# Mamba's state loop in a four-image network: the input of both halves in one VectorE instruction, two sets of tiles, new turn tables

## Chip, cores, metric

The kernel runs on one core of one Trainium2 chip. The metric is the time of one execution on the device, in microseconds. The time before is 1499.15 us, the median of 3 runs (1498.88 to 1500.82).

## What is computed

The input is a batch of 4 images of 512 tokens with 128 features, in float32. Eight residual layers follow each other: a state-space mixer (L0), a feed-forward layer, a Mamba block, a mixture of 8 experts with GELU, a linear attention, a ternary feed-forward layer, a second state-space scan, and a gated mixture of 8 experts. Each is applied as x = x + layer(layernorm(x)). What the change touches is the Mamba block, cut here to its state loop:

```python
D_STATE = 16; D_INNER = 256
u, z = split(layernorm(x) @ W_in); u = silu(conv1d(u) + conv_b)
dt, Bm, Cm = split(u @ W_xproj)            # widths 8, 16, 16
dt = softplus(dt @ W_dt + b_dt)
A = -exp(A_log)                            # (256, 16)
dA = exp(dt[..., None] * A)                # decay, for each token, channel, state
dBu = (dt * u)[..., None] * Bm[:, :, None, :]   # input of the state
h = dA_t * h + dBu_t                       # over the tokens
y_t = sum over n of h[:, n] * C_t[n]
out = x + ((y + u * D) * silu(z)) @ W_out
```

## The kernel before

**Streams.** Four images are worked off in two streams: images 0 and 2 are stream 0, images 1 and 3 are stream 1. Each stream has its own tiles (suffix `s`) and four of the eight PSUM banks (`bank(s, k)`, L465). Each engine's program is written as Python generators, one per layer and image, which yield between pieces of work. `walk` (L483) asks the two streams' generators for their next piece in the order of a fixed table: `RUNS[engine]` (L100 to L142) holds run lengths, alternately for stream 0 and stream 1. So the order of all instructions on an engine's queue is written out ahead, the two streams are interleaved by the table, and a piece that has to wait holds up everything behind it on that engine. The table `"sp"` does the same for the expert loads, stores and gathers of the SyncE queue, and `expert_loads` (L164) reads from it in which order the ring of four expert buffers is filled.

**Mamba, by engine.** The channels lie on the partitions in two halves j = 0, 1 of 128, the 512 tokens on the free axis. Per image, 16 iterations n (one for each state) follow the preparation:

- TensorE (`mamba`, from L1620): broadcasts row n of Bm to bank 2 and row n of Cm to bank 3 (L1659, a 96-row selection matmul in bf16). `sum_states` (L1638) adds the weighted states of both halves onto banks 0 and 1 with the identity as weights (L1642), over all n.
- ScalarE (`mamba`, from L782): copies bank 2 to the tile MT in SBUF (L814), and computes the decays of the two halves into CV (L821, Exp with the scale A).
- GpSimd (`mamba`, L614): multiplies MT with dt*u of half 1 into BIG2[1] (L624).
- VectorE (`mamba`, from L1192): multiplies bank 2 with dt*u of half 0 into BIG2[0] (L1222), then runs the scans of both halves into UP (L1230), then multiplies both with bank 3 into BIG2[2:4] (L1237, 128x1024 in one instruction, the PSUM row broadcast over the halves).

There is one set of decay tiles (CV) and one of input tiles (BIG2[0:2]). So the exponential of state n + 1 waits for the scan of state n of the same half, and the input of state n + 1 for that scan too. The semaphores: `m_bc` counts TensorE's rows, `m_bs` the copies, `m_da` the decays, `m_d1` GpSimd's products, `m_scan` VectorE's four instructions of an iteration, `m_ya` the sums.

**Around it.** The layers that can run beside Mamba are the L0 mixer of the other stream (VectorE convolutions L1050 to L1053, gates L1084; TensorE L1529) and the experts (TensorE L1739 up and L1712 down, ScalarE's GELU L862, VectorE's results L1314, GpSimd's indirect DMAs L639 for the scatter and L646 for the gather). GpSimd also computes the norms' power (L587). ScalarE loads a function table whenever the function set changes (Exp, Ln, Silu, Gelu, Sigmoid).

## Time and profile before

| what | value |
|---|---|
| runs | 1499.15 us median, 1498.88 to 1500.82 |
| profiled execution, its own time | 1508.51 us |
| its span, first to last instruction | 1506.4 us |
| mean granted TensorE clock | 0.886 |
| instructions | 16451 |
| HBM traffic | 109.31 MB read, 15.07 MB written |

The profile is of one execution. A busy time is the time in which an engine has an instruction under way; times of instructions are starts and durations by the hardware profiler, and durations of neighbours on VectorE overlap by some tens of ns. "Idle before" is the time in which the engine stood still ahead of such an instruction, put down to what released it last. L numbers are lines of the kernel before. The tile names leave buffer numbers out: `big` is BIG1 or BIG2, `ps` is PSUM, `mt`, `cv`, `up`, `q` are MT, CV, UP and the split rows. The stretches of the Mamba loops below run from the first to the last scan: image 0's from 216.3 to 316.8 us, image 1's from 259.7 to 389.2, image 2's from 879.6 to 990.4, image 3's from 1033.3 to 1116.6.

### The profile page before, as it was taken

What the parts mean: (1) busy time and instruction counts of PE and PEld (TensorE: products, weight loads), DVE (VectorE), ACT (ScalarE), POOL (GpSimd) and SP (SyncE); (2) the same over time, 40 slices, a digit from 0 to 9 for tenths busy, and PEclk for the clock granted to TensorE, in tenths of its full rate; (3) what the DMA queues carried; (4) which work ended last, traced back from release to release, by engine and by line L of the source; (5) the groups of instructions that cost most, each with busy time, mean ns of one, the idle gap of its engine ahead of it and who ended that gap; (6) DMA issues with size and microseconds to landing.
All of it is one profiled execution on the core that took longest, in us unless ns stands there. A gap on an engine that the chain in (4) does not pass through costs nothing.

```text
span 1506.4 us, 16451 instructions
## 1 busy us (share of the span) xinstructions
PE 1151.1 (76%) x5428; PEld 761.0 (51%) x5428; DVE 920.1 (61%) x2079; ACT 662.9 (44%) x1289; POOL 280.6 (19%) x261
## 2 busy tenths in 40 slices
PE   0988656667869989976897767755867999978774
PEld 0534522233757446666775423433635745547674
DVE  4575679998627384234484778987786355334432
ACT  1532267524634343452452476436943434443321
POOL 1200112425140201203202211213242020020222
PEclk9998767877989998989999868986988999988987
DMA  8000000003564000536540000003513600033763
GB/s 330 0 1 0 1 0 0 0 1 103 188 200 125 20 1 4 172 101 212 172 166 28 7 0 0 0 1 104 172 43 104 200 15 1 0 131 121 271 205 131
DMA packets 57641, 125.50 MB, mean 83 GB/s; under 512 B 5320, under 2 KB 38224, under 8 KB 57168
## 3 DMA queue, kind: packets, MB, share of 16 engines
q1 hardware_dynamic: 52880, 111.14, 22.5%
q0 software_dynamic: 4096, 8.40, 1.7%
q10 hardware_dynamic: 576, 4.87, 0.8%
q8 instruction: 45, 0.74, 0.2%
q14 instruction: 44, 0.36, 0.1%
HBM read 109.31 MB, written 15.07 MB: 83 GB/s over the span
## 4 chain that ended last, share of the span: by engine, by line
PE 46%; DVE 18%; ACT 13%; issue 9%; DMA 8%; POOL 5%; SPq 1%; DVEq 0%; another core or an unknown queue 0%; POOLq 0%; ACTq 0%
PE ps L1739 6%; PE ps L1801 5%; PE ps L1529 5%; DMA expert_ring<-in_e_dram 4%; PE ps L1477 4%; PE ps L1642 3%; PE ps L1712 3%; DVE up L1230 3%; PE ps L1771 2%; POOL slots_dram L639 2%; POOL up L646 2%; PE ps L1582 2%; PE ps L1839 1%; ACT big L862 1%; PE ps L1790 1%
## 5 line engine op out<-in xcount | busy, mean ns | idle before, releaser
L1739 PE MATMUL ps<-big,expert_ring 128*128 128x128 f32 x1440 | 200.1, 289 | 45.6 <-DMA expert_ring<-in_e_dram 18.1
L1739 PEld LDWEIGHTS ps<-big,expert_ring 128*128 128x128 f32 x1440 | 184.6, 201 | 66.7 <-issue 34.5
L587 POOL TENSOR_TENSOR rstd<-ve,nhalf 128x4 f32<-128x4 f32 x44 | 48.2, 1096 | 692.3 <-DVE ve L1024 548.0
L1230 DVE TENSOR_TENSOR_SCAN up<-cv,big 128x512 f32<-128x512 f32 x128 | 151.5, 1223 | 24.7 <-ACT cv L821 18.1
L1642 PE MATMUL ps<-big,consts 128*128 128x512 f32 x256 | 149.1, 713 | 2.2 <-DVE big L1237 2.2
L1712 PE MATMUL ps<-expert_ring,big 128*128 128x128 f32 x960 | 130.0, 279 | 11.5 <-DVE big L1350 6.4
L624 POOL TENSOR_TENSOR big<-big,mt 128x512 f32<-128x512 f32 x64 | 85.1, 1333 | 263.2 <-ACT mt L814 133.6
L1712 PEld LDWEIGHTS ps<-expert_ring,big 128*128 128x128 f32 x960 | 119.3, 194 | 18.4 <-DVE big L1350 7.1
L1659 PE MATMUL ps<-q,row_pick 96*128 96x512 bf16 x128 | 54.5, 441 | 89.3 <-DVE big L1237 57.4
L1801 PE MATMUL ps<-big,weights 128*128 128x512 f32 x256 | 116.1, 598 | 0.8 <-DVE big L1402 0.8
L859 ACT ACTIVATE key<-ps,expert_ring 128x128 f32<-128x128 f32 x240 | 68.6, 369 | 106.2 <-PE ps L1739 94.6
L1350 DVE SCALAR_TENSOR_TENSOR big<-ps,expert_ring,key 128x128 f32<-128x128 f32 x240 | 67.5, 344 | 67.2 <-PE ps L1739 48.8
L1477 PE MATMUL ps<-weights,big 128*128 128x128 f32 x608 | 83.6, 298 | 16.3 <-DVE big L1244 10.5
L821 ACT ACTIVATE cv<-big,nega 128x512 f32<-128x512 f32 x128 | 88.1, 716 | 16.6 <-DVE up L1230 16.0
L1477 PEld LDWEIGHTS ps<-weights,big 128*128 128x128 f32 x608 | 79.5, 210 | 29.1 <-DVE big L1244 13.7
L639 POOL DMA_INDIRECT slots_dram<-cv,key x64 | 66.8, 1044 | 122.2 <-DVE key L1301 105.5
L814 ACT ACTIVATE mt<-ps 128x512 f32<-128x512 f32 x64 | 38.2, 599 | 114.6 <-PE ps L1659 104.8
L862 ACT ACTIVATE big<-ps,expert_ring 128x128 f32<-128x128 f32 x240 | 68.3, 376 | 44.6 <-PE ps L1739 44.4
L646 POOL DMA_INDIRECT up<-results_dram,key x64 | 62.1, 970 | 126.2 <-DMA results_dram<-mt 101.4
L1642 PEld LDWEIGHTS ps<-big,consts 128*128 128x128 f32 x256 | 58.5, 230 | 50.0 <-issue 42.6
L1659 PEld LDWEIGHTS ps<-q,row_pick 96*128 96x128 bf16 x128 | 13.4, 106 | 135.9 <-DVE big L1237 74.0
L1237 DVE TENSOR_TENSOR big<-up,ps 128x1024 f32<-128x1024 f32 x64 | 77.6, 1213 | 7.0 <-PE ps L1642 6.1
(249 smaller groups left out, 1990.7 us busy)
## 6 DMA issues: line engine op xcount, KB each, us to landing
expert_ring<-in_e_dram SPq DMA_DIRECT2D x60, 836.0 KB
expert_ring<-in_e_dram SPq DMA_DIRECT2D x60, 578.0 KB
big<-slots_dram SPq DMA_DIRECT2D x24, 256.0 KB, 3.2
results_dram<-mt SPq DMA_DIRECT2D x24, 256.0 KB, 4.5
weights<-in_w_dram ACTq DMA_DIRECT2D x1, 3072.0 KB, 14.8
slots_dram<-big SPq DMA_DIRECT2D x2, 960.0 KB, 16.0
weights<-in_w_dram SPq DMA_DIRECT2D x1, 1600.0 KB, 13.4
big<-slots_dram SPq DMA_DIRECT2D x8, 192.0 KB, 3.8
```

The source lines that it names most:

```text
L624: pool.tensor_tensor(BIG2[s][:, 1, :], BIG1[s][:, 3, :], MT[s][:, 0:T], ALU.mult).then_inc(m_d1[s], 1)
L639: pool.indirect_dma_start(xs_d[k], bass.IndirectOffsetOnAxis(ap=posu[s][:, j:j + 1], axis=0), XH[s][:, j % NC, :], None).then_inc(scattere ...
L646: pool.indirect_dma_start(YG[s][:, j // NC, (j % NC) * P:(j % NC + 1) * P], None, ys_d[k], bass.IndirectOffsetOnAxis(ap=posu[s][:, j:j + 1 ...
L821: act.activation(CV[s][:, j, :], BIG1[s][:, j, :], ACT.Exp, scale=nega[:, j * NM + n:j * NM + n + 1]).then_inc(m_da[s], 1)
L862: last = act.activation(HID[s][:, b % 4, cols], bank(s, b % 2)[:, cols], ACT.Gelu, bias=bias[:, k:k + 1])
L1230: dve.tensor_tensor_scan(UP[s][:, j, PAD:PAD + T], CV[s][:, j, :], BIG2[s][:, j, :], 0.0, ALU.mult, ALU.add).then_inc(m_scan[s], 1)
L1237: dve.tensor_tensor(BIG2[s][:, 2:4, :], UP[s][:, :, PAD:PAD + T], bank(s, 3).unsqueeze(1).broadcast_to([P, 2, T]), ALU.mult).then_inc(m_sc ...
L1477: last = pe.matmul(bank4(s, k)[:, c, :], lhs(b, c), rhs(b), start=(b == 0), stop=(b == blocks - 1))
L1642: pe.matmul(bank(s, j), ident, BIG2[s][:, 2 + j, :], start=(n == 0), stop=(n == NM - 1))\
L1712: last = pe.matmul(bank4(s, 2 + b % 2)[:, 0, :], HID[s][:, b % 4, k * P:(k + 1) * P], wd[:, k * P:(k + 1) * P], start=(k == 0), stop=(k == 3))
L1739: last = pe.matmul(bank4(s, r if m else b % 2)[:, k, :], ring[:, q % RING, r * T + k * P:r * T + (k + 1) * P], XGT[s][:, b // 4, b % 4 * P ...
L1801: last = pe.matmul(bank(s, j), w(name, (4 * b + j) * P, P), BIG1[s][:, src + b, :], start=(b == 0), stop=(b == 3))
```

## The change

- VectorE forms the input of both halves with one instruction, bank 2 broadcast over the halves times BIG1[2:4]. GpSimd's product L624 and ScalarE's copy L814 leave, with their semaphores.
- There are two sets of input tiles (`DBU`: BIG2[0:2] and 1024 columns of KEY) and two of decay tiles (`DA`: CV, and for odd states parts of MT and XT). The exponential of state n waits for the scan of state n - 2.
- On VectorE the order in an iteration is: scan of half 0, scan of half 1, input of state n + 1, weighting of state n. The first scan waits for the weighting of state n - 1.
- The row for the input of state n waits only for the input product of state n - 1.
- An iteration has one piece of work less on each of TensorE, ScalarE, VectorE and GpSimd, and all five turn tables are new (the diff shows "pool" and "sp" in full, of "pe" the first line; "act" and "dve" are replaced in the same way).

```diff
--- before.py
+++ after.py
@@ -99,46 +99,44 @@
 RUNS = {
     "pe": [
-        1, 1, 1, 1, 1, 1, 8, 1, 4, 5, 2, 2, 2, 2, 2, 2, 5, 4, 2, 2, 2, 2, 1, 1, 2, 6, 30, 1, 10, 2, 1, 9, 1,
+        1, 2, 1, 1, 1, 2, 8, 1, 4, 5, 2, 2, 2, 2, 2, 2, 5, 4, 2, 2, 2, 2, 1, 1, 2, 5, 2, 2, 38, 2, 1, 23, 1,
...
     "pool": [
-        1, 1, 1, 1, 1, 1, 1, 1, 3, 2, 1, 1, 5, 1, 2, 1, 2, 1, 2, 1, 2, 1, 2, 2, 1, 2, 5, 1, 2, 1, 1, 14, 10,
-        9, 1, 1, 10, 11, 11, 8, 1, 2, 11, 1, 6, 1, 1, 2, 9, 15, 2, 1, 7, 9, 1, 10, 7, 1, 4, 10, 8, 8],
+        1, 2, 1, 1, 2, 1, 1, 1, 2, 2, 17, 1, 1, 8, 1, 9, 1, 1, 10, 1, 9, 2, 1, 8, 4, 14, 18, 9, 1, 9, 1, 1,
+        10, 11, 8, 8],
     "sp": [
-        1, 1, 21, 2, 2, 21, 22, 2, 1, 6, 1, 16, 23, 23, 21, 1, 1, 7, 1, 5, 1, 11],
+        1, 1, 23, 23, 24, 24, 23, 23, 21, 1, 1, 1, 1, 7, 1, 15],
 }
@@ -230,6 +228,8 @@
         factored = sb("factored", [P, 1])
         ones64 = sb("ones64", [N0, P])
         negr = [sb(f"negr{s}", [N3, 8]) for s in range(NS)] * ROUNDS
+        DBU = [[BIG2[s][:, 0:2, :], KEY[s][:, T:3 * T].rearrange("p (j n) -> p j n", j=2)] for s in range(NB)]
+        DA = [[[CV[s][:, 0, :], MT[s][:, T:2 * T]], [CV[s][:, 1, :], XT[s][:, PAD:PAD + T]]] for s in range(NB)]
         XG = BIG2
         XGT = [BIG1[s][:, 0:4, :] for s in range(NB)]
         HID = [BIG1[s][:, 4:8, :] for s in range(NB)]
@@ -363,12 +363,20 @@
         m_uz_s = S("act", 4)
         m_d8 = S("act", 1)
         m_sp = S("act", 2)
-        m_bs = S("act", NM)
         m_da = S("act", 2 * NM)
         m_cv = S("dve", 2)
         m_mix = S("dve", 5)
         m_scan = S("dve", 4 * NM)
-        m_d1 = S("pool", NM)
+
+        def input_made(n):
+            return 4 * n - 1 if n else 0
+
+        def scanned(n, j):
+            return 4 * n + 1 + j
+
+        def weighted(n):
+            return 4 * n + 3 + (n < NM - 1)
+
 
         moe = []
 
@@ -614,14 +622,6 @@
             def mamba(s):
                 yield from ln(n2o, s)
                 yield from ln(n2, s)
-                for n in range(NM):
-                    yield
-                    pool.wait_ge(m_bs[s], m_bs.at(s, n))
-                    if n == 0:
-                        pool.wait_ge(m_mix[s], m_mix.at(s, 2))
-                    else:
-                        pool.wait_ge(m_scan[s], m_scan.at(s, 4 * n - 2))
-                    pool.tensor_tensor(BIG2[s][:, 1, :], BIG1[s][:, 3, :], MT[s][:, 0:T], ALU.mult).then_inc(m_d1[s], 1)
 
             def plain(layer):
 
@@ -807,18 +807,13 @@
                 for j in range(2):
                     act.activation(CV[s][:, j, :], CV[s][:, j, :], ACT.Ln, bias=1.0).then_inc(m_sp[s], 1)
                 for n in range(NM):
-                    yield
-                    act.wait_ge(m_bc[s], m_bc.at(s, 2 * n))
-                    if n:
-                        act.wait_ge(m_d1[s], m_d1.at(s, n - 1))
-                    act.activation(MT[s][:, 0:T], bank(s, 2), ACT.Copy).then_inc(m_bs[s], 1)
                     for j in range(2):
                         yield
-                        if n == 0:
+                        if n < 2:
                             act.wait_ge(m_mix[s], m_mix.at(s, 1 + j))
                         else:
-                            act.wait_ge(m_scan[s], m_scan.at(s, 4 * n - 3 + j))
-                        act.activation(CV[s][:, j, :], BIG1[s][:, j, :], ACT.Exp,
+                            act.wait_ge(m_scan[s], m_scan.at(s, scanned(n - 2, j)))
+                        act.activation(DA[s][j][n % 2], BIG1[s][:, j, :], ACT.Exp,
                                        scale=nega[:, j * NM + n:j * NM + n + 1]).then_inc(m_da[s], 1)
 
             def route(g, s):
@@ -1216,21 +1211,27 @@
                     step(dve.tensor_tensor(BIG1[s][:, j, :], CV[s][:, j, :], UP[s][:, j, PAD:PAD + T], ALU.add))
                     dve.tensor_tensor(BIG1[s][:, 2 + j, :], BIG1[s][:, j, :], BIG1[s][:, 4 + j, :], ALU.mult)\
                         .then_inc(m_mix[s], 1)
+                def state_input(n):
+                    yield
+                    dve.wait_ge(m_bc[s], m_bc.at(s, 2 * n))
+                    if n == 0:
+                        dve.wait_ge(m_mix[s], m_mix.at(s, 2))
+                    dve.tensor_tensor(DBU[s][n % 2], bank(s, 2).unsqueeze(1).broadcast_to([P, 2, T]), BIG1[s][:, 2:4, :],
+                                      ALU.mult).then_inc(m_scan[s], 1)
+
+                yield from state_input(0)
                 for n in range(NM):
-                    yield
-                    dve.wait_ge(m_bs[s], m_bs.at(s, n))
-                    dve.tensor_tensor(BIG2[s][:, 0, :], bank(s, 2), BIG1[s][:, 2, :], ALU.mult).then_inc(m_scan[s], 1)
-                    yield
-                    dve.wait_ge(m_scan[s], m_scan.at(s, 4 * n))
                     for j in range(2):
                         yield
                         dve.wait_ge(m_da[s], m_da.at(s, 2 * n + j))
-                        if j:
-                            dve.wait_ge(m_d1[s], m_d1.at(s, n))
-                        dve.tensor_tensor_scan(UP[s][:, j, PAD:PAD + T], CV[s][:, j, :], BIG2[s][:, j, :], 0.0,
+                        if j == 0:
+                            dve.wait_ge(m_scan[s], m_scan.at(s, weighted(n - 1) if n else input_made(0)))
+                        dve.tensor_tensor_scan(UP[s][:, j, PAD:PAD + T], DA[s][j][n % 2], DBU[s][n % 2][:, j, :], 0.0,
                                                ALU.mult, ALU.add).then_inc(m_scan[s], 1)
-                    yield
-                    dve.wait_ge(m_scan[s], m_scan.at(s, 4 * n + 2))
+                    if n < NM - 1:
+                        yield from state_input(n + 1)
+                    yield
+                    dve.wait_ge(m_scan[s], m_scan.at(s, scanned(n, 1)))
                     dve.wait_ge(m_bc[s], m_bc.at(s, 2 * n + 1))
                     if n:
                         dve.wait_ge(m_ya[s], m_ya.at(s, 2 * n - 1))
@@ -1637,24 +1638,19 @@
 
                 def sum_states(n):
                     yield
-                    pe.wait_ge(m_scan[s], m_scan.at(s, 4 * n + 3))
+                    pe.wait_ge(m_scan[s], m_scan.at(s, weighted(n)))
                     for j in range(2):
                         pe.matmul(bank(s, j), ident, BIG2[s][:, 2 + j, :], start=(n == 0), stop=(n == NM - 1))\
                             .then_inc(m_ya[s], 1)
 
                 for n in range(NM):
-                    yield
-
-                    if n == 0:
-                        pe.wait_ge(m_mix[s], m_mix.at(s, 0))
-                        pe.wait_ge(m_sp[s], m_sp.at(s, 1))
                     for k in range(2):
                         yield
-                        if n and k == 0:
-                            pe.wait_ge(m_scan[s], m_scan.at(s, 4 * n - 4))
-                            pe.wait_ge(m_bs[s], m_bs.at(s, n - 1))
+                        if n == 0 and k == 0:
+                            pe.wait_ge(m_mix[s], m_mix.at(s, 0))
+                            pe.wait_ge(m_sp[s], m_sp.at(s, 1))
                         elif n:
-                            pe.wait_ge(m_scan[s], m_scan.at(s, 4 * n - 1))
+                            pe.wait_ge(m_scan[s], m_scan.at(s, weighted(n - 1) if k else input_made(n - 1)))
                         r = 16 * k + n
                         pe.matmul(bank(s, 2 + k), SM[:, r:r + 1].broadcast_to([96, P]), SPL[s][:, :],
                                   start=True, stop=True).then_inc(m_bc[s], 1)
```

## Rows read from the trace of the kernel before

**Rows 1.** The page's first part: busy us, share of the span, instructions.

```profile
PE 1151.1 (76%) x5428; PEld 761.0 (51%) x5428; DVE 920.1 (61%) x2079; ACT 662.9 (44%) x1289; POOL 280.6 (19%) x261
```

**Rows 2.** The page's chain that ended last, share of the span by engine, by line.

```profile
PE 46%; DVE 18%; ACT 13%; issue 9%; DMA 8%; POOL 5%; SPq 1%; DVEq 0%; another core or an unknown queue 0%; POOLq 0%; ACTq 0%
PE ps L1739 6%; PE ps L1801 5%; PE ps L1529 5%; DMA expert_ring<-in_e_dram 4%; PE ps L1477 4%; PE ps L1642 3%; PE ps L1712 3%; DVE up L1230 3%; PE ps L1771 2%; POOL slots_dram L639 2%; POOL up L646 2%; PE ps L1582 2%; PE ps L1839 1%; ACT bi
```

**Rows 3.** Busy us by stretch: length, PE, PEld, DVE, ACT, POOL; clock, DMA, GB/s.

```profile
216.30:259.70 43.40, 25.48 (x55) 10.27 (x56) 39.84 (x49) 30.21 (x43) 11.43 (x8) 0.78 0.00 0
259.70:316.80 57.10, 38.14 (x85) 14.96 (x84) 57.10 (x59) 26.38 (x42) 20.73 (x15) 0.86 0.00 0
316.80:389.20 72.40, 51.87 (x200) 29.76 (x198) 60.68 (x101) 33.32 (x61) 25.81 (x19) 0.79 0.24 77
879.60:990.40 110.80, 82.45 (x270) 41.84 (x270) 98.21 (x126) 60.00 (x85) 22.16 (x18) 0.85 0.00 1
1033.30:1116.60 83.30, 66.29 (x345) 44.83 (x344) 67.32 (x77) 64.55 (x124) 26.04 (x22) 0.92 0.39 121
```

**Rows 4.** The page's groups: busy us, mean ns, idle before, its cause.

```profile
L1230 DVE TENSOR_TENSOR_SCAN up<-cv,big 128x512 f32<-128x512 f32 x128 | 151.5, 1223 | 24.7 <-ACT cv L821 18.1
...
L624 POOL TENSOR_TENSOR big<-big,mt 128x512 f32<-128x512 f32 x64 | 85.1, 1333 | 263.2 <-ACT mt L814 133.6
...
L821 ACT ACTIVATE cv<-big,nega 128x512 f32<-128x512 f32 x128 | 88.1, 716 | 16.6 <-DVE up L1230 16.0
...
L814 ACT ACTIVATE mt<-ps 128x512 f32<-128x512 f32 x64 | 38.2, 599 | 114.6 <-PE ps L1659 104.8
...
L1237 DVE TENSOR_TENSOR big<-up,ps 128x1024 f32<-128x1024 f32 x64 | 77.6, 1213 | 7.0 <-PE ps L1642 6.1
```

**Rows 5.** Single lines: duration ns, min/median/max, first and last start.

```profile
L1230 DVE TENSOR_TENSOR_SCAN up<-cv,big x128: 1185/1204/2580, 216.3 to 1115.4; 128x512 f32<-128x512 f32 x128
...
L1222 DVE TENSOR_TENSOR big<-ps,big x64: 653/683/692, 214.3 to 1113.5; 128x512 f32<-128x512 f32 x64
```

**Rows 6.** VectorE's waits, us, times, longest: 216 to 390 us, then 879 to 1117.

```profile
DVE up L1230 <- POOL big L624: 3.4, 1, 3.4
...
DVE up L1230 <- ACT cv L821: 2.7, 2, 1.8
...
DVE up L1230 <- ACT cv L821: 15.4, 12, 3.3
...
DVE big L1237 <- PE ps L1642: 4.7, 6, 1.3
...
DVE up L1230 <- POOL big L624: 2.4, 1, 2.4
```

**Rows 7.** VectorE's timeline from 257 us: start, duration, instruction, idle time before.

```profile
257.92 1.21 DVE L1237 TENSOR_TENSOR big<-up,ps 128x1024 f32<-128x1024 f32 x1
259.05 0.68 DVE L1222 TENSOR_TENSOR big<-ps,big 128x512 f32<-128x512 f32 x1
259.65 4.56 DVE L1230 TENSOR_TENSOR_SCAN up<-cv,big 128x512 f32<-128x512 f32 x4
```

**Rows 8.** VectorE's timeline in image 3's loop, same columns.

```profile
1089.14 2.34 DVE L1230 TENSOR_TENSOR_SCAN up<-cv,big 128x512 f32<-128x512 f32 x2 [2.12 <-ACT cv L821]
...
1092.71 0.68 DVE L1222 TENSOR_TENSOR big<-ps,big 128x512 f32<-128x512 f32 x1
...
1093.42 2.34 DVE L1230 TENSOR_TENSOR_SCAN up<-cv,big 128x512 f32<-128x512 f32 x2
```

**Rows 9.** ScalarE's lines from 1033.3 to 1116.6 us, columns as in Rows 4.

```profile
L814 ACT ACTIVATE mt<-ps 128x512 f32<-128x512 f32 x15 | 9.1, 607 | 13.0 <-PE ps L1659 9.9 <-POOL big L624 3.1
...
L862 ACT ACT_TABLE_LOAD x7 | 9.0, 1283 | 0.1
...
L821 ACT ACT_TABLE_LOAD x7 | 9.0, 1283 | 0.1
```

**Rows 10.** Busy us from 1050 to 1100 us, columns as in Rows 3.

```profile
1050.00:1100.00 50.00, 44.99 (x261) 32.60 (x260) 40.69 (x50) 47.36 (x94) 11.49 (x9) 1.00 0.48 147
```

62 rows, old and new, of the table RUNS are left out of this document.

## The prediction

> **What bounds the kernel now.** I read five views, from coarse to fine. First the busy times [rows 1]: TensorE works for 76% of the span, VectorE for 61%, ScalarE for 44%, GpSimd for 19%. No engine is full, so a mean decides nothing. Then the chain of work that ended last [rows 2]: 46% of it is TensorE, 18% VectorE, 5% GpSimd. Its GpSimd lines are the indirect DMAs of the experts (L639, L646); the Mamba product L624 is not among its leading lines. So taking that product away gives nothing by itself. Then the four Mamba loops one by one [rows 3]. The profile gives 43.4 + 57.1 + 72.4 us in which the loops of images 0 and 1 run, and 110.8 and 83.3 us for images 2 and 3. There VectorE is the fullest engine: 39.84 of 43.4 us, 57.10 of 57.1, 60.68 of 72.4, then 98.21 of 110.8. In the last loop it is 67.32 of 83.3, with ScalarE at 64.55. TensorE's granted clock is 0.78 to 0.86 of full in all but the last of these, so part of each at its lower level (1.2 of 2.4 GHz); I carry the matmul times over as they are. The change acts only here, so the sum is made from these stretches. The groups [rows 4], the durations of single lines [rows 5], the waits [rows 6] and two stretches of VectorE's timeline [rows 7, 8] give the prices.
>
> **The change, part by part.** The sum is against the profiled execution (span 1506.4 us, its own time 1508.51 us). The median of the three runs is 1499.15 us, 0.6% lower, and I lay the difference on the median.
>
> *VectorE's input product.* Each of 64 iterations (4 images x 16 states) now multiplies the broadcast row in PSUM with both halves in one 128x1024 instruction, in place of 128x512. The old one has a median of 683 ns [rows 5]. The new one isn't in the trace; L1237 has its shape and its mix of one PSUM operand broadcast over two halves and one in SBUF: 1213 ns [rows 4]. From below I bound it by 683 (a second half for nothing), from above by two of the old ones, 1366 ns; I take 1213. What counts is the step to the next instruction: when nothing waits, L1222 at 259.05 is followed after 0.60 us, L1237 at 257.92 after 1.13 us [rows 7]. So one iteration costs 0.53 us more: 64 x 0.53 = 34 us of VectorE.
>
> *A self-wait that goes.* Where a stream has VectorE to itself, today the first scan waits for the input product directly in front of it, and the weighting (L1237) waits for the second scan directly in front of it. L1222 at 1092.71 is followed after 0.71 us, not 0.60 [rows 8]. The change puts the next input product between the second scan and the weighting, and then the first scan waits for the weighting directly in front: of two such waits one is left. That gives back 0.11 us per iteration without a neighbour. By the new VectorE table image 0 finishes Mamba when image 1 has had 23 of its 75 turns; 9 of these precede the loop and an iteration has 4, so 3.5 iterations are shared. Before, it was (39 - 9) / 5 = 6. So about 12 iterations of image 1 run without another loop beside them, and the 16 of image 3: 28 x 0.11 = 3 us back, 1.3 in round 0 and 1.8 in round 1.
>
> *GpSimd.* 64 products leave, 85.1 us [rows 4]. They are hidden today, except where VectorE waited for them: 3.4 us in one wait in the first two loops, 2.4 in the last two [rows 6]. GpSimd's queue is in order, so the expert scatters of one image stand behind the products of the other; those products wait for a row and a scan of theirs. The chain's share of L639 is 2%, and I credit nothing for it; from below it is nothing, from above that whole share, some 30 us of the span, which no wait in the rows supports.
>
> *ScalarE.* 64 copies of 599 ns leave, 38.2 us [rows 4]. In the last loop this matters: there ScalarE is busy for 47.36 of the 50 us from 1050 [rows 10], since GELUs of image 2's experts alternate with the exponentials, with 14 table loads of 1.283 us, and 15 copies of 9.1 us together [rows 9]. One scan pair starts 2.12 us late because of it [rows 8]. The second pair of decay tiles lets the exponentials of state n+1 run during the scans of state n. The waits of the scans on L821, 15.4 us in the last two loops and 2.7 in the first two [rows 6], are what may go. Against it: counting the changes of function set along ScalarE's new order gives 108, with 94 in the old one; 9 pairs instead of 7 lie in the last loop. 14 more loads x 1.283 = 18 us, beside other work unless ScalarE leads a chain. In the last loop: 9.1 us of copies less, 4 loads more (5.1 us), so 60.5 us of ScalarE, no longer the bound.
>
> *TensorE.* The matmuls stay. The row product of the next state waits for the current input product alone, no longer for ScalarE's copy too. Behind that wait on TensorE's queue stand the row for the weighting and, by the tables, work of the other stream; the input product is now early in the iteration, so I cost the wait at nothing. If its cover is gone, VectorE waits one row product, about 0.4 us, per iteration. L1237's wait for TensorE, 4.7 us in the last two loops [rows 6], stays.
>
> *Tables and SP.* SP's table now runs each stream's expert loads nearly as whole layers. I find no added load, and cost the rest of the tables at nothing from both sides of zero: below and above I allow 8 us, half of VectorE's 16 us of idle time in the last loop, the nearest measure in the rows of what an order leaves unused.
>
> *Sum per stretch* [rows 3]. Loops of images 0 and 1: 172.9 us with 157.6 busy, 15.3 idle. Added 32 x 0.53 - 1.3 = 15.7, which is as long as all the idle time, so 173.3 us is a floor. I keep half of the idle time (the waits on ScalarE and GpSimd are 6.1 us of it): 157.6 + 15.7 + 7.6 = 180.9, **+8.0 us**. Image 2: 110.8 with 98.2 busy; 98.2 + 8.5 + half of 12.6 = 113.0, **+2.2**. Image 3: 83.3 with 67.3 busy; 67.3 + 8.5 - 1.8 + half of 16.0 = 82.0, **-1.3**. Together +8.9. Of the 8.0 us by which image 1 comes late I take 2 as covered, because its expert loads stand behind image 0's in SP's table. That leaves +7: **1506 us**.
>
> *A rule weighed against a row.* The scans have a median of 1204, a maximum of 2580 and a mean of 1223 ns [rows 4, 5]: over the median they lose 128 x 19 ns = 2.4 us in all. The Trainium skill ("SBUF — State Buffer", "SBUF: two separate sides") says that GpSimd and a VectorE instruction with two SBUF inputs take an exclusive lock for a whole instruction. By it the removal is a gain, and what it could be here at most is rival 3. The rows show that such blocks are few; I leave the 2.4 us out of the sum.
>
> **The rivals.**
> 1. *The idle time is not shared out again.* If the waits stay and the whole 34 - 3 = 31 us land on the path: **1530 us**. For it: the stretch of 57.1 us has no idle time at all. Against it: the last loop was held by ScalarE. Chance 0.11.
> 2. *Faster.* The scan's idle time, 24.7 us [rows 4], goes because the exponentials run a state ahead, and the last loop sheds its ScalarE bound; with L1237's 7.0 and the allowance of 8 us for the tables that is 40 against 31, less the 2 us that are covered: 1499 + 31 - 40 - 2, **1488 us**. It decides at the scan: once VectorE's idle time in the four loops falls from 44 us (15.3 + 12.6 + 16.0) below 13, the added 31 us are paid. For it: the last two loops hold 28.6 us of idle time, most of the scan's waits. Against it: the first two have only 15.3 us to give. Chance 0.32.
> 3. *The lock is the price.* All of the scan's 24.7 us of idle time and its 2.4 us over the median are GpSimd's doing: 1506 - 27 = **1479 us**. Against it: the waits name ScalarE, whose queue is seen full [rows 9, 10]. Chance 0.04. It is the mechanism that the Trainium skill's page "SBUF — State Buffer" describes.
> 4. *No difference.* The added work goes exactly into idle time, or the change doesn't do what it says, because the new order doesn't use the second tiles: within 3 us of **1499 us**. The tables speak against the latter: ScalarE has runs of 4, 6 and 8 exponentials of one image, where 2 was the rule. Chance 0.15.
>
> **How the numbers follow.** The forecast, 0.38, covers +3 to +20 us around 1506, so 1502 to 1519 by itself. 0.2% is 3 us, about what a measurement of this kernel can tell from no change. Slower: 0.38 + 0.11 = 0.49; same 0.15; faster 0.32 + 0.04 = 0.36. The range reaches down past rival 2 to 1483 and up to 1528, near rival 1; outside lie rival 3 and the ends of rivals 1 and 2, 2 in 10.
>
> **What would show it.** Right: 64 input products of about 1.2 us, VectorE's busy time near 920 + 34 = 954 us, ScalarE's copies gone and about 14 more table loads, the scan's wait on L821 mostly gone, and image 3's loop no longer than 83 us while those of images 0 and 1 take about 181 us. Wrong: an input product far from 1.2 us; loops of images 0 and 1 under 174 us; or loops as summed and the change found elsewhere, in the expert layers, which would say that the tables weigh more than the loop.

## The result: 1527.89 us, 1.8% slower, and the profile after

The changed kernel takes 1527.89 us, the median of 4 runs (1518.96 to 1531.70); the kernel before took 1499.02 us (1498.21 to 1500.82) beside it. The ratio is 1.0182, with a 95% interval of 1.0131 to 1.0234. The forecast was +7 us, 1506 us; what came is +29 us, beyond the 1502 to 1519 that the forecast was to cover by itself. The range 1483 to 1528 holds the result by 0.1 us, which is luck, and the sign is right. Its reason, as the runs below show, is not. One execution of e1 (6170.58 us) and one of the kernel before beside e9 to e11 (3886.04 us) lie far off; they count in the medians and not in the ratios.

The page's first part, of the changed kernel:

```profile
PE 1177.8 (77%) x5428; PEld 764.9 (50%) x5428; DVE 946.9 (62%) x2079; ACT 648.4 (42%) x1239; POOL 195.9 (13%) x197
```

Against [rows 1], VectorE is busy for 26.8 us more (I had said 34), GpSimd for 84.7 us less, and ScalarE for 14.5 us less. TensorE has the same 5428 matmuls and is busy for 26.7 us more, at a mean granted clock of 0.871 where it was 0.886: it ran at its lower level (1.2 of 2.4 GHz) for longer. The profiled execution took 1531.70 us, 23.2 more than the one before.

The stretches of the loops, cut again from first to last scan (columns as in [rows 3]):

```profile
211.30:257.60 46.30, 27.08 (x47) 9.37 (x47) 41.62 (x45) 26.61 (x36) 0.00 (x0) 0.73 0.00 1
257.60:313.30 55.70, 39.09 (x65) 14.09 (x65) 49.09 (x45) 13.72 (x19) 0.00 (x0) 0.67 0.00 0
313.30:416.10 102.80, 78.86 (x371) 51.96 (x372) 77.23 (x122) 47.04 (x98) 10.48 (x10) 0.79 0.36 111
883.90:1021.20 137.30, 99.26 (x334) 50.63 (x334) 115.71 (x145) 69.30 (x91) 8.53 (x7) 0.88 0.00 0
1064.50:1146.10 81.60, 67.48 (x345) 45.07 (x345) 74.39 (x77) 61.26 (x111) 6.34 (x7) 0.92 0.41 124
```

Images 0 and 1 take 46.3 + 55.7 + 102.8 = 204.8 us where it was 172.9, image 2 takes 137.3 where it was 110.8, image 3 takes 81.6 where it was 83.3. In the second stretch VectorE had no idle time at all before; now it is idle for 6.6 of 55.7 us, although its loop has more to do. The groups of the loop's lines name what for (line, shapes, count | busy us, mean ns | idle us before, its cause; L1219 is the input product, L1229 the scans, L1238 the weighting, L1655 the row products, L1643 the sums):

```profile
L1238 DVE TENSOR_TENSOR big<-up,ps 128x1024 f32<-128x1024 f32 x64 | 77.4, 1211 | 2.8 <-PE ps L1643 2.8
...
L1229 DVE TENSOR_TENSOR_SCAN up<-cv,big 128x512 f32<-128x512 f32 x64 | 74.9, 1209 | 0.9
...
L1219 DVE TENSOR_TENSOR big<-ps,big 128x1024 f32<-128x1024 f32 x32 | 39.1, 1221 | 17.5 <-PE ps L1655 17.3
...
L1219 DVE TENSOR_TENSOR key<-ps,big 128x1024 f32<-128x1024 f32 x32 | 39.0, 1218 | 16.8 <-PE ps L1655 16.6
...
L1229 DVE TENSOR_TENSOR_SCAN up<-mt,key 128x512 f32<-128x512 f32 x32 | 38.9, 1217 | 1.0
...
L1229 DVE TENSOR_TENSOR_SCAN up<-xT,key 128x512 f32<-128x512 f32 x32 | 38.4, 1201 | 0.0
```

The waits of the scans for the exponentials are gone: 1.9 us of idle time before the scans, where it was 24.7 [rows 4]. In their place stands a wait that the kernel before did not have: **34.3 us before the input product, for TensorE's row product L1655**. VectorE's waits from 211 to 417 us (total us, times, longest) hold 21.2 us of it:

```profile
DVE key L1219 <- PE ps L1655: 11.0, 10, 2.1
DVE big L1219 <- PE ps L1655: 10.2, 9, 2.1
```

One turn of it, from the timeline of the changed kernel (start us, duration us, engine, line; idle time before in brackets; image 0's loop, with one input product of image 1 at 271.36):

```profile
269.09 1.22 DVE L1219 TENSOR_TENSOR key<-ps,big 128x1024 f32<-128x1024 f32 x1 [1.18 <-PE ps L1655]
...
270.23 1.21 DVE L1238 TENSOR_TENSOR big<-up,ps 128x1024 f32<-128x1024 f32 x1
...
271.36 1.22 DVE L1219 TENSOR_TENSOR key<-ps,big 128x1024 f32<-128x1024 f32 x1
...
271.50 0.61 PE L1655 MATMUL ps<-q,row_pick 96*128 96x512 bf16 x1 [2.45 <-DVE big L1238]
...
271.90 3.62 PE L1643 MATMUL ps<-big,consts 128*128 128x512 f32 x4
...
272.49 1.21 DVE L1229 TENSOR_TENSOR_SCAN up<-mt,key 128x512 f32<-128x512 f32 x1
...
273.62 1.20 DVE L1229 TENSOR_TENSOR_SCAN up<-xT,key 128x512 f32<-128x512 f32 x1
...
275.31 0.63 PE L1655 MATMUL ps<-q,row_pick 96*128 96x512 bf16 x1
...
275.98 1.23 DVE L1219 TENSOR_TENSOR big<-ps,big 128x1024 f32<-128x1024 f32 x1 [1.16 <-PE ps L1655]
...
277.12 2.34 DVE L1238 TENSOR_TENSOR big<-up,ps 128x1024 f32<-128x1024 f32 x2
```

Read it as a ring. The weighting of state n (L1238, 270.23) ends at 271.44. Only then may TensorE overwrite bank 3 and add up: the row for the next weighting at 271.50, then the two sums from 271.90, four passes of 3.62 us together (ends on TensorE are modelled, and overlap the next start). Behind them in TensorE's queue stands the row for the input, 275.31 to 275.94. VectorE has finished both scans at 274.8 and waits 1.16 us; the input product starts at 275.98, and the next weighting, which now stands *behind* the input product, at 277.12. 277.12 - 270.23 = 6.89 us: the input product and the weighting are links of the same ring as the sums.

### The profile page after: what moved, and what is told of

Its sections match the earlier page's. It is cut to its first block, busy times and chain, and to the rows that moved or that the text cites. A ratio compares the mean times of both kernels' runs of the same rounds, so it can differ in the third digit from the quotient of the medians.

```text
span 1529.9 us, 16093 instructions
## 1 busy us (share of the span) xinstructions
PE 1177.8 (77%) x5428; PEld 764.9 (50%) x5428; DVE 946.9 (62%) x2079; ACT 648.4 (42%) x1239; POOL 195.9 (13%) x197
## 4 chain that ended last, share of the span: by engine, by line
PE 51%; DVE 20%; ACT 9%; DMA 8%; issue 6%; POOL 4%; SPq 1%; DVEq 0%; POOLq 0%; ACTq 0%
PE ps L1643 7%; PE ps L1735 7%; DMA expert_ring<-in_e_dram 5%; PE ps L1530 5%; PE ps L1797 4%; PE ps L1478 4%; PE ps L1708 4%; DVE big L1238 3%; PE ps L1583 2%; DVE up L1229 2%; PE ps L1655 2%; PE ps L1835 2%; POOL up L646 1%; POOL slots_dram L639 1%; PE ps L1767 1%
## 5 line engine op out<-in xcount | busy, mean ns | idle before, releaser
L1735 PE MATMUL ps<-big,expert_ring 128*128 128x128 f32 x1440 | 193.8, 284 | 33.0 <-DMA expert_ring<-in_e_dram 16.4
L1735 PEld LDWEIGHTS ps<-big,expert_ring 128*128 128x128 f32 x1440 | 178.6, 196 | 52.3 <-DMA expert_ring<-in_e_dram 24.7
L1643 PE MATMUL ps<-big,consts 128*128 128x512 f32 x256 | 162.3, 769 | 6.3 <-DVE big L1238 6.3
L1655 PE MATMUL ps<-q,row_pick 96*128 96x512 bf16 x128 | 58.2, 469 | 101.4 <-DVE big L1238 80.5
L1643 PEld LDWEIGHTS ps<-big,consts 128*128 128x128 f32 x256 | 62.1, 244 | 60.2 <-issue 46.6
L1655 PEld LDWEIGHTS ps<-q,row_pick 96*128 96x128 bf16 x128 | 13.8, 110 | 155.1 <-DVE big L1238 107.5
L1478 PEld LDWEIGHTS ps<-weights,big 128*128 128x128 f32 x608 | 78.2, 209 | 21.8 <-DVE big L1245 12.6
L1238 DVE TENSOR_TENSOR big<-up,ps 128x1024 f32<-128x1024 f32 x64 | 77.4, 1211 | 2.8 <-PE ps L1643 2.8
L1767 PE MATMUL ps<-qkv_parts,selectors_rounded 128*128 128x512 f32 x192 | 73.4, 501 | 7.0 <-DVE up L1388 4.1
L1797 PEld LDWEIGHTS ps<-big,weights 128*128 128x128 f32 x256 | 47.5, 190 | 57.1 <-issue 53.0
L1530 PE MATMUL ps<-big,mt 128*128 128x512 f32 x160 | 73.5, 616 | 3.0 <-ACT big L723 3.0
L1229 DVE TENSOR_TENSOR_SCAN up<-cv,big 128x512 f32<-128x512 f32 x64 | 74.9, 1209 | 0.9
```

What stands on the lines that cost most here:

```text
L1229: dve.tensor_tensor_scan(UP[s][:, j, PAD:PAD + T], DA[s][j][n % 2], DBU[s][n % 2][:, j, :], 0.0, ALU.mult, ALU.add).then_inc(m_scan[s], 1)
L1238: dve.tensor_tensor(BIG2[s][:, 2:4, :], UP[s][:, :, PAD:PAD + T], bank(s, 3).unsqueeze(1).broadcast_to([P, 2, T]), ALU.mult).then_inc(m_sc ...
L1478: last = pe.matmul(bank4(s, k)[:, c, :], lhs(b, c), rhs(b), start=(b == 0), stop=(b == blocks - 1))
L1530: last = pe.matmul(bank(s, c), MT[s][:, m:m + P], BIG2[s][:, k, :], start=(k == 0), stop=(k == c))
L1643: pe.matmul(bank(s, j), ident, BIG2[s][:, 2 + j, :], start=(n == 0), stop=(n == NM - 1))\
L1655: pe.matmul(bank(s, 2 + k), SM[:, r:r + 1].broadcast_to([96, P]), SPL[s][:, :], start=True, stop=True).then_inc(m_bc[s], 1)
```

## The experiments

Theory A is that ring. Theory B is my prediction's: the added VectorE work. Theory C: the new tables. All times are compared as ratios to the kernel before on the same chip (the ratios as recorded; they differ from those of the medians by up to 0.15%), whose median was 1496.2 us beside e1 to e4, 1509.3 beside e5 to e8, 1499.7 beside e9 to e11. "Loop idle" is VectorE's idle time before scans, input products and weightings.

| run | ratio (95%) | VectorE busy us | loop idle us |
|---|---|---|---|
| before | 1 | 920.1 | 31.8 |
| changed kernel | 1.0182 (1.0131 to 1.0234) | 946.9 | 39.0 |
| e1 row ahead | 1.0049 (1.0025 to 1.0073) | 944.6 | 13.0 |
| e2 old tables | 1.0189 (1.0149 to 1.0229) | 945.0 | 37.1 |
| e3 half input | 1.0000 (0.9980 to 1.0019) | 913.8 | 35.4 |
| e4 old tables, row ahead | 1.0100 (1.0062 to 1.0138) | 944.0 | 23.5 |
| e5 row ahead, half input | 0.9915 (0.9884 to 0.9946) | 913.9 | 24.3 |
| e6 old tables, one decay set | 1.0202 (1.0142 to 1.0261) | 945.7 | 38.2 |
| e7 input after weighting | 0.9990 (0.9959 to 1.0020) | 948.0 | 11.6 |
| e8 before, two decay sets | 0.9983 (0.9961 to 1.0006) | 920.8 | 30.3 |
| e9 input after weighting, old tables | 0.9988 (0.9967 to 1.0009) | 945.5 | 11.6 |
| e10 input after weighting, row ahead | 1.0163 (1.0103 to 1.0224) | 947.5 | 36.6 |
| e11 input after weighting, half input | 0.9969 (0.9941 to 0.9998) | 915.5 | 21.5 |

### e1: the row ahead of the sums

```diff
+                yield from row(0, 0)
                 for n in range(NM):
-                    for k in range(2):
...
+                    yield from row(1, n)
+                    if n < NM - 1:
+                        yield from row(0, n + 1)
                     if n:
                         yield from sum_states(n - 1)
```

`row(k, n)` is the old body of the loop over k (wait and matmul), put into a function; the removed body is cut here.

> The changed kernel, with TensorE's row product for the input of the next state moved ahead of the two sums of the state before (same tables, same waits). Theory A (the row stands behind the sums in TensorE's queue, and VectorE's input product waits for it): the 34 us of idle time before the input product fall below 8 us, and the time falls from 1528 by 15 to 30 us, to 1498 to 1513. Theory B (the 27 us of added VectorE work are the loss): the idle time goes and the time stays within 6 us of 1528, since the work only moves. Theory C (the new tables cost it): within 6 us of 1528, and the idle time before the input product turns into idle time before other streams' pieces.

Measured: 1504.32 us, ratio 1.0049. The lines of VectorE:

```profile
L1238 DVE TENSOR_TENSOR big<-up,ps 128x1024 f32<-128x1024 f32 x64 | 77.5, 1213 | 10.5 <-PE ps L1643 10.1
...
L1219 DVE TENSOR_TENSOR big<-ps,big 128x1024 f32<-128x1024 f32 x32 | 38.6, 1207 | 0.5 <-PE ps L1654 0.2
...
L1219 DVE TENSOR_TENSOR key<-ps,big 128x1024 f32<-128x1024 f32 x32 | 38.5, 1202 | 0.1
```

The idle time before the input product is gone (0.6 us) and the time with it, 1.3% or 20 us. That is A's number; B and C both said within 6 us of 1528. 10.5 us now stand before the weighting instead, for the sums.

### e2: the old tables

The changed loop, in the tables of before without the turns of the pieces that left.

> The changed loop with the turn tables of the kernel before, from which only the turns of the pieces that left are taken out. Theory C (the new tables cost it): the time falls to about 1500 to 1508, image 1's loop takes about 130 us as before and not 158. Theory A: the row stands behind the sums here too, so the idle time before the input product stays over 25 us and the time stays over 1520. Theory B: 1520 to 1535, with little idle time before the input product.

Measured: 1526.06 us, ratio 1.0189, the same as with the new tables.

```profile
L1228 DVE TENSOR_TENSOR_SCAN up<-cv,big 128x512 f32<-128x512 f32 x64 | 74.6, 1207 | 5.3 <-ACT cv L815 3.9
...
L1228 DVE TENSOR_TENSOR_SCAN up<-mt,key 128x512 f32<-128x512 f32 x32 | 39.0, 1218 | 6.4 <-ACT mt L815 5.0
...
L1218 DVE TENSOR_TENSOR big<-ps,big 128x1024 f32<-128x1024 f32 x32 | 38.9, 1218 | 12.6 <-PE ps L1654 12.2
...
L1218 DVE TENSOR_TENSOR key<-ps,big 128x1024 f32<-128x1024 f32 x32 | 38.8, 1212 | 11.0 <-PE ps L1654 10.8
```

The tables are not the cost: C falls. 23.6 us before the input product stay; A had said over 25. The scans wait 11.7 us here and 1.9 with the new tables. So these do place the exponentials better, but the end gains nothing from it here. Image 1's loop takes 142 us, not 130. The fourth combination, the loop of before in the new tables, was not tried: their order of ScalarE's exponentials and VectorE's input products doesn't fit its waits.

### e3: half the input product

```diff
-                    dve.tensor_tensor(DBU[s][n % 2], bank(s, 2).unsqueeze(1).broadcast_to([P, 2, T]), BIG1[s][:, 2:4, :],
-                                      ALU.mult)
+                    dve.tensor_tensor(DBU[s][n % 2][:, 0, :], bank(s, 2), BIG1[s][:, 2, :], ALU.mult)
...
-                        dve.tensor_tensor_scan(UP[s][:, j, PAD:PAD + T], DA[s][j][n % 2], DBU[s][n % 2][:, j, :], 0.0,
+                        dve.tensor_tensor_scan(UP[s][:, j, PAD:PAD + T], DA[s][j][n % 2], DBU[s][n % 2][:, 0, :], 0.0,
```

> The changed kernel with the input product of half 0 alone (128x512 in place of 128x1024); both scans read it, so the input of half 1 is left out. VectorE has some 34 us less to do, all else is the same. Theory B (the added VectorE work is the loss): 1528 minus 25 to 34 us, 1494 to 1503. Theory A: VectorE comes to its wait for the row earlier and waits longer; the idle time before the input product grows from 34 us to over 50, and the time stays over 1515. Theory C: over 1520.

Measured: 1498.31 us, ratio 1.0000: 27 us less, B's number, and **my expectation for A missed**. The idle time did not grow:

```profile
L1219 DVE TENSOR_TENSOR big<-ps,big 128x512 f32<-128x512 f32 x32 | 21.9, 686 | 16.8 <-PE ps L1654 16.5
...
L1219 DVE TENSOR_TENSOR key<-ps,big 128x512 f32<-128x512 f32 x32 | 21.9, 683 | 15.1 <-PE ps L1654 15.1
```

31.9 us, where it was 34.3. I had taken the row's time as fixed from outside, so that a faster VectorE would only wait longer. But a link of a ring is not beside it: a shorter input product starts the weighting earlier, that the sums, and those the next row. The wait per turn stays, and each turn is 0.53 us shorter; 64 x 0.53 = 34 us is the most that this can give, 27 came. So e1 and e3 together don't separate A from B. What does is to take the input product out of the ring at full width.

### e7: the input product after the weighting

VectorE's order as in the kernel before: scan, scan, weighting of n, input of n + 1. New tables, rows behind the sums.

```diff
-                            dve.wait_ge(m_scan[s], m_scan.at(s, weighted(n - 1) if n else input_made(0)))
+                            dve.wait_ge(m_scan[s], m_scan.at(s, input_made(n)))
...
-                    if n < NM - 1:
-                        yield from state_input(n + 1)
                     yield
                     dve.wait_ge(m_scan[s], m_scan.at(s, scanned(n, 1)))
...
+                    if n < NM - 1:
+                        yield from state_input(n + 1)
```

The counts `input_made` and `weighted` are changed to match.

> The changed kernel (new tables, rows behind the sums), but on VectorE the input product of the next state comes after the weighting, as before the change, not ahead of it. Theory A in its sharper form (the change moved the input product one weighting, 1.13 us, closer to the weighting that lets TensorE go on, and the row for it stands behind that): the idle time before the input product falls from 34 to under 12 us, while some 3 us come back from self-waits, and the time falls to 1500 to 1514. If the place on VectorE doesn't matter: within 6 us of 1528.

Measured: 1509.44 us beside 1509.34 of the kernel before, ratio 0.9990. By the ratios that is 29 us less than the changed kernel, one more than A's most. All of the 1.8% is back, with all of the added VectorE work (948.0 us busy).

```profile
L1236 DVE TENSOR_TENSOR big<-up,ps 128x1024 f32<-128x1024 f32 x64 | 77.9, 1219 | 9.5 <-PE ps L1643 8.0
...
L1219 DVE TENSOR_TENSOR key<-ps,big 128x1024 f32<-128x1024 f32 x32 | 39.0, 1217 | 0.0
...
L1219 DVE TENSOR_TENSOR big<-ps,big 128x1024 f32<-128x1024 f32 x32 | 38.8, 1218 | 0.2
```

The same place in its timeline, VectorE alone:

```profile
270.45 1.22 DVE L1236 TENSOR_TENSOR big<-up,ps 128x1024 f32<-128x1024 f32 x1
271.59 1.22 DVE L1219 TENSOR_TENSOR big<-ps,big 128x1024 f32<-128x1024 f32 x1
272.73 1.22 DVE L1219 TENSOR_TENSOR key<-ps,big 128x1024 f32<-128x1024 f32 x1
273.86 2.33 DVE L1229 TENSOR_TENSOR_SCAN up<-cv,big 128x512 f32<-128x512 f32 x2
276.22 1.22 DVE L1236 TENSOR_TENSOR big<-up,ps 128x1024 f32<-128x1024 f32 x1
277.36 1.22 DVE L1219 TENSOR_TENSOR key<-ps,big 128x1024 f32<-128x1024 f32 x1
```

From one weighting of image 0 (270.45) to the next (276.22) it is 5.77 us, against 6.89, and the input products start without a wait: by the time of the input of n + 1, the weighting of n stands between it and the scans, and TensorE has had 1.13 us more for its sums. That is about the 1.16 us by which VectorE was late. Both spans hold one input product of image 1 and no scan of it.

### e4, e5: do the parts add?

e4 is e2 with e1's edit; e5 is e1 with e3's.

> Old tables (as in the run before) and the row ahead of the sums together. Theory A: 10 to 30 us less than with the old tables alone. Theory B: no less than that within 6 us, and both near 1528. Theory C: near 1500 to 1508 in both. If A and C each hold in part, this is the fastest of the four, below 1500.

> The changed kernel with the row ahead of the sums and with half 0's input alone (half 1's input is left out). It says whether the two prices add: each alone gave 24 us and 30 us. If they are separate (the wait for the row, and VectorE's own time): near 1475. If they are one slack seen from two sides (VectorE faster only waits more for the rows and sums on TensorE): 1488 to 1500, with over 15 us of idle time before the weighting.

Measured: e4 1510.96 us, ratio 1.0100, 0.9% or 13 us under e2, as A said; the old tables leave 12.3 us before the scans. Against e1 this is the one pair in which the tables tell: with the row ahead, the new ones are 0.5% or 8 us faster (1.0049 and 1.0100, intervals that barely overlap), for 10.4 us less idle time before the scans. e5: 1497.01 us, ratio 0.9915. It is 1.3% or 20 us under e1 and lies between my two cases: of 30.7 us of VectorE work that leave, 11.3 turn into idle time (13.0 to 24.3 us), most of it 21.8 us before the weighting. 0.9915 is the lowest ratio of the study, but half of the input is left out.

### e6, e8: the second set of decay tiles

e6 is e2 with one set, and its exponential waits for the scan of n - 1; e8 is the kernel before with two, all else kept. Two lines of e8's edit:

```diff
-                        act.activation(CV[s][:, j, :], BIG1[s][:, j, :], ACT.Exp,
+                        act.activation(DA[s][j][n % 2], BIG1[s][:, j, :], ACT.Exp,
```

> The changed loop with the old tables, and one set of decay tiles in place of two. If the second set is worth what the scan's wait for the exponentials was before (24.7 us idle), the time rises from 1526 by 8 to 20 us. If the tables, not the tiles, place the exponentials, it stays within 5 us of 1526.

> The kernel before, GpSimd's product and all tables kept, with the second set of decay tiles alone. If the scan's waits for the exponentials come from the single set: 5 to 12 us less than before, 1485 to 1494. If they come from ScalarE's written order and its full queue in image 3's loop: within 4 us of 1499.

Measured: e6 1541.48 us, ratio 1.0202, against 1.0189 for e2, its second case, with 11.7 us of idle time before the scans in both. The intervals of the two are wide enough to hide some 10 us either way. e8: 1505.04 us, ratio 0.9983 with an interval that holds 1; idle before the scans 23.2 us, where it was 24.7. Under the old tables the second set is worth nothing that these runs can tell. That the written order of ScalarE says when an exponential runs, and the tiles only allow it to be earlier, fits that and was not tested by itself. (e6's time of 1541 us is not comparable with e2's 1526: the kernel before was 13 us slower on that chip too.) What the new tables would lose with one set was not tried.

### e9, e10, e11: around e7

e9 is e7's loop in the old tables, e10 is e7 with e1's edit, e11 is e7 with e3's (half 1's input left out).

> The changed loop with the input product after the weighting (the order on VectorE before the change) and the old tables: the pure move of GpSimd's and ScalarE's share to VectorE. Measured on ratios to the kernel before: new tables with this order gave 0.999. If the new tables bring nothing, 0.997 to 1.002 here too. If the move costs VectorE time (34 us of work, less the waits that leave) and the new tables pay for it elsewhere (VectorE's wait for the gathered results was 34 us with the new tables and 63 to 67 with the old): 1.007 to 1.02.

> Both cures together, new tables: input product after the weighting, and the row ahead of the sums. If the loop's wait was the only thing that either cures, the second adds nothing, or costs up to 1%, since the row now waits for an input product that comes after the weighting and holds the sums: ratio 0.999 to 1.01. If the sums still delay the rows, 0.985 to 0.995, which beats the kernel before.

> Input product after the weighting, new tables, and half 0's input alone (half 1's input is left out): the price of VectorE's added 34 us where no input product waits for a row. If VectorE bounds the loops there: 20 to 34 us less than with both halves, a ratio of 0.977 to 0.986. If the idle time before the weighting takes it up: 0.990 or more.

e9: 1497.03 us, ratio 0.9988. That is the first case of its expectation: with the input product after the weighting, the new tables bring nothing over the old ones that can be told.

```profile
L1235 DVE TENSOR_TENSOR big<-up,ps 128x1024 f32<-128x1024 f32 x64 | 77.6, 1213 | 4.2 <-PE ps L1642 3.3
...
L1228 DVE TENSOR_TENSOR_SCAN up<-cv,big 128x512 f32<-128x512 f32 x64 | 74.6, 1207 | 3.0 <-ACT cv L815 1.6
...
L1218 DVE TENSOR_TENSOR big<-ps,big 128x1024 f32<-128x1024 f32 x32 | 38.9, 1214 | 0.3
```

Its loops, cut from first to last scan like [rows 3] (images 0 and 1, image 2, image 3):

```profile
217.10:392.00 174.90, 118.32 (x343) 55.90 (x344) 167.65 (x205) 72.51 (x114) 12.98 (x10) 0.81 0.09 30
881.40:993.70 112.30, 83.79 (x272) 42.80 (x272) 104.60 (x127) 50.95 (x70) 2.86 (x2) 0.86 0.00 0
1036.60:1115.30 78.70, 67.37 (x345) 44.84 (x345) 74.86 (x77) 55.34 (x107) 7.24 (x7) 0.91 0.41 129
```

That is the cleanest price of the move itself, since tables (less the turns of the pieces that left) and VectorE's order are those of before: 174.9 us for 172.9, 112.3 for 110.8, 78.7 for 83.3. VectorE is busy for 167.65 of the 174.9 us, so the added work went into what was idle time. With the input product ahead of the weighting (e2, same tables) the first of these stretches is 189.6 us.

e10: 1523.45 us, ratio 1.0163, worse than I had allowed. Each cure alone works and both together undo it:

```profile
L1236 DVE TENSOR_TENSOR big<-up,ps 128x1024 f32<-128x1024 f32 x64 | 78.0, 1220 | 34.5 <-PE ps L1643 33.7
...
L1219 DVE TENSOR_TENSOR key<-ps,big 128x1024 f32<-128x1024 f32 x32 | 38.9, 1216 | 0.0
```

The row now waits for an input product that comes after the weighting, and the sums stand behind the row; 34.5 us of idle time stand before the weighting, which waits for them. It is the same ring by another link.

e11: 1492.83 us, ratio 0.9969, 3 us under e7 by the ratios and 4 us under e9, its neighbour on the same chip. Both cases of my expectation were stated as sizes, and the second holds: it is over 0.990. VectorE lost 32.5 us of work against e7; 9.9 us of it became idle time, most in the one group of the weighting:

```profile
L1235 DVE TENSOR_TENSOR big<-up,ps 128x1024 f32<-128x1024 f32 x64 | 77.9, 1219 | 19.4 <-PE ps L1642 18.3
```

The intervals of e7 and e11 overlap, so the price of the added VectorE work in this order is somewhere from nothing to 9 us, no longer 27. Where the rest of the freed time goes was not followed.

**Taken together.** VectorE's busy time and its loop idle time added up are 951.9 us before and 985.9 after: 34.0 us more, for 29 us of the medians. The same sum says e1 +5.7, e2 +30.2, e3 -2.7, e4 +15.6, e5 -13.7, e6 +32.0, e8 -0.8 us; the ratios give +7, +28, 0, +15, -13, +30, -3. With the input product after the weighting it does worse: for e7, e9 and e11 (+7.7, +5.2, -14.9) they give -2, -2, -5, and for e10 +32.2 they give +24. So the sum explains the runs in the changed kernel's order within 3 us, and misses by 7 to 10 us in the other. No version is clearly faster than the kernel before at full computation; e7, e8 and e9 are the nearest, with 1 inside their intervals.

## Why the prediction was right and wrong, step by step

- **Input product, 1213 ns from L1237: right** (1221 and 1218 ns). **VectorE +34 us of busy time: 26.8.** The durations of the input products rose by 34.6 us (43.5 to 78.1), as summed. All other VectorE instructions are 3.1 us shorter together, and neighbours overlap by 4.7 us more, which the busy time counts once.
- **What binds: right in part.** With the input product ahead of the weighting, a shorter VectorE instruction does shorten the execution, which e3 and e5 show; in e11, with the other order, 30 us less work gave only 3 to 5 us. And the added work was not what cost 1.8%. e7 and e9 carry all of it at 0.999: the loops' idle time fell from 31.8 to 11.6 us, which pays for 20 of the 25 to 28 us; what pays for the rest was not found. Stretch by stretch e9 has +2.0, +1.5 and -4.6 us for my +8.0, +2.2 and -1.3. The floor of 173.3 us for images 0 and 1 was not passed, and it was nearly reached (174.9); that half of the idle time would stay was the guess that made the work too dear.
- **TensorE, "I cost the wait at nothing", and 0.4 us per iteration if its cover is gone: this step failed.** I listed what stands behind the waiting row, but not what stands in front of it: two sums of 1.8 us each at the lower clock level, that themselves wait for the weighting. The wait was 33.8 us in 33 cases, 1.0 us each, where 0.4 us in every iteration would be 26. "I carry the matmul times over as they are" failed too: for the same 5428 matmuls TensorE was busy for 26.7 us more. Of the moved input product I asked what it lets go earlier (a self-wait, 3 us) and not what it now needs earlier.
- **ScalarE: right on the waits, wrong on their cause.** The idle time before the scans fell by 22.8 us, of the 24.7 I had for rival 2, and image 3's loop is 81.6 us for a forecast of 82.0. e6 and e8 show that this is not the second set's doing alone: with the old tables it is 11.7 us in the changed loop, with two sets or one, so what left with the copies and GpSimd's products, or the new order on VectorE, took 13 us, and the new tables the rest. Its count of instructions is 1289 to 1239, that is 64 copies less and 14 table loads more, as counted.
- **Tables at nothing within 8 us: right,** but not in every version: they differ by 0.1% in either order (e2 and the changed kernel, e9 and e7), and by 0.5% once the row is ahead (e4 and e1). **GpSimd's products at nothing:** no run takes them away alone; e9, which does it with the work moved to VectorE, is at 0.9988.
- **Stretches as measured in the changed kernel:** images 0 and 1 were 204.8 for 180.9 us, image 2 137.3 for 113.0. Only a part of that is loss: e7, with the new tables and 0.2 us of waits before the input product, still has 188.3 us (212.5 to 400.8) and 135.1 us (864.2 to 999.3). The new tables put more of the other stream's layers beside these loops, and give it back elsewhere. So a stretch that I had named as the test of my sum was no test of it once the tables changed.
- **Rivals:** rival 1 had the time, 1530, by another mechanism, and rival 2's mechanism came true (waits gone, ScalarE no bound) and was outweighed. I had no rival with a new wait in it, though the change moved an instruction across the one that lets another engine go on.

## What to carry to other kernels

When an instruction is moved in front of another on its in-order engine, follow the ring: what does the one that now comes later release, on which queue does that work stand, and what does the moved one need from that queue? Here an input product moved ahead by 1.13 us met a row behind two sums, waited for it in 33 of 64 turns, and cost 29 us; moving it back heals it, moving the row ahead of the sums heals most of it (1.0049), and both at once bring a ring back (1.0163). A link of such a ring also makes a "work" experiment deceptive: shortening it gains like a bound engine, with the wait unchanged.

## What the runs showed of the hardware that I had not expected

**TensorE's clock differed with the order.** In the second stretch, in one profile each, the granted clock was 0.67 of full in the changed kernel and 0.86 in the kernel before [rows 3], with nearly the same TensorE work in it (39.09 and 38.14 us busy); in the same stretch of e7 it was 0.86 again with 30.02 us busy, and in e1 0.70 with 36.13. At the lower level (1.2 GHz of 2.4) the four passes of the two sums take 3.62 us in the timeline above (granted clock 0.50 there); at the higher one the same four take 1.88 us (1.00), in e7 at 277.96 and in the changed kernel itself at 285.73. e1's loop is as short as e7's there (49.1 and 49.5 us) at the lower clock, so with the row ahead the low clock cost this stretch nothing. With the row behind the sums it did: of the 33 waits of the input product in the changed kernel, 18 end a stretch of 4.5 us with a granted clock of 0.50 to 0.66 and make up 22.9 us, 1.3 us each; the other 15 (0.94 to 1.00) make up 11.0 us, 0.7 us each. So the ring is there at both levels, and two thirds of its wait fell where the clock was low. Whole executions at the same granted clock still differ: spans of 1521.2 to 1529.0 us in e2 at 0.877 to 0.880, and 1502.0 us of the kernel before on that chip at 0.878. No run holds the clock fixed, and which of the two an order will get is not shown.

**GpSimd's products had lengthened a few other VectorE instructions.** Convolution steps L1051, in the kernel before and (as L1046) in the changed one, min/median/max ns:

```profile
L1051 DVE SCALAR_TENSOR_TENSOR cv<-up,params,cv x40: 750/752/1635, 56.3 to 1013.5; 128x512 f32<-128x512 f32 x40
```

```profile
L1046 DVE SCALAR_TENSOR_TENSOR cv<-up,params,cv x40: 750/752/754, 57.2 to 1045.1; 128x512 f32<-128x512 f32 x40
```

The same holds for the scans, whose longest was 2580 ns [rows 5]:

```profile
L1229 DVE TENSOR_TENSOR_SCAN up<-cv,big x64: 1198/1209/1226, 211.3 to 1138.4; 128x512 f32<-128x512 f32 x64
```

The longest of each, in the kernel before, stands beside a product of GpSimd:

```profile
232.95 1.42 POOL L624 TENSOR_TENSOR big<-big,mt 128x512 f32<-128x512 f32 x1 [5.68 <-DVE up L1230]
```

```profile
233.28 1.64 DVE L1051 SCALAR_TENSOR_TENSOR cv<-up,params,cv 128x512 f32<-128x512 f32 x1
```

and likewise the long pair of scans at 359.70 (3.69 us) beside a product at 359.91. e8, which keeps the products, has the 2580 ns scan too. Summed, it was worth little: the 128 scans together take 152.2 us after, 151.5 before, and all VectorE instructions but the input products are 3.1 us shorter. The Trainium skill ("SBUF — State Buffer", "SBUF: two separate sides") says that GpSimd and a VectorE instruction with two SBUF inputs exclude each other for a whole instruction; these two collisions agree with it. Most of the 64 products ran beside the weighting or the input product, which read one operand from PSUM; no L1222 took more than 692 ns [rows 5], no L1237 more than 1222.
